# Last stage of a one-core transformer kernel: another order of its first units, registers loaded by group, gathers a unit sooner

## The reference

```python
logits = xt @ gate_w.T
scores = softmax(logits)
_, idx = top_k(scores + gate_b, 2)
weights = take_along_axis(scores, idx)             # dw: zero but for the two chosen experts
h = silu(einsum('td,eid->tei', xt, W1)) * einsum('td,eid->tei', xt, W3)     # 8 experts, 128 wide
y = einsum('tei,edi,te->td', h, W2, dw)
z = silu(xt @ Ws1.T) * (xt @ Ws3.T) @ Ws2.T        # a shared expert for all tokens
x = x + 0.5 * (y + z)
```

## Time and profile before

| | us |
|---|---|
| median of three runs | 1614.95 |
| the profiled execution, its own time | 1613.27 |
| its span from first to last instruction | 1611.3 |
| last stage, from up(0) to the end | 124 (1487.3 to 1611.3) |
| last matmul begins | 1606.4 |
| last DVE instruction ends | 1608.3 |

### The profile page before, as it was taken

One profiled execution on the slowest core, in us unless ns is written; L12 is line 12 of the kernel. 1 busy time (PEld: TensorE's weight loads), 2 busy tenths in 40 slices (PEclk: granted clock), 3 DMA queues, 4 the chain that ended last, 5 costly groups with the idle time before them and its releaser, 6 DMA issues. The chain is left out here.

```text
span 1611.3 us, 26807 instructions
## 1 busy us (share of the span) xinstructions
PE 1557.1 (97%) x9214; PEld 905.7 (56%) x9214; DVE 1245.2 (77%) x2324; ACT 1214.3 (75%) x1904; POOL 1167.9 (72%) x823
## 2 busy tenths in 40 slices
PE   3998899999999999999999999999999999999898
PEld 2566445555555555555555555555567566688575
DVE  7888777777777777777777778778888886988627
ACT  7876888989989998998898888887655543345442
POOL 0865888888888898888888888887575322476535
PEclk9999999999999999999999999999999999999999
DMA  9311879889779889879889887887401430000433
GB/s 310 128 54 41 141 140 170 144 144 180 150 151 168 155 153 168 158 144 169 164 146 165 152 159 142 159 153 137 84 1 33 129 83 4 1 1 8 107 98 98
DMA packets 641371, 197.10 MB, mean 122 GB/s; under 512 B 601547, under 2 KB 639062, under 8 KB 640982
## 3 DMA queue, kind: packets, MB, share of 16 engines
q1 hardware_dynamic: 636662, 188.19, 59.8%
q0 software_dynamic: 1536, 4.20, 0.8%
q10 hardware_dynamic: 3040, 3.02, 0.6%
HBM read 36.71 MB, written 10.22 MB: 29 GB/s over the span
## 5 line engine op out<-in xcount | busy, mean ns | idle before, releaser
L970 POOL TENSOR_TENSOR Pl<-Pm,Ph 128x1024 f16<-128x1024 f32 x256 | 545.9, 2132 | 43.8 <-ACT Ph L1311 43.5
L1301 ACT ACTIVATE Pm<-banks,nbias,s_scale 128x1024 f32<-128x1024 f32 x256 | 307.6, 1202 | 96.3 <-DVE nbias L1944 95.3
L1942 DVE TENSOR_REDUCE nmax<-banks 128x1 f32<-128x1024 f32 x256 | 311.7, 1218 | 88.3 <-PE banks L2517 87.8
L1311 ACT ACTIVATE Ph<-Pm 128x1024 f16<-128x1024 f32 x256 | 268.1, 1047 | 1.5
L949 POOL TENSOR_TENSOR rp_b<-rp_s,rope 128x512 f32<-128x512 f32 x128 | 163.1, 1274 | 98.7 <-ACT rp_s L1278 97.2
L1975 DVE SCALAR_TENSOR_TENSOR X<-banks,rinv,X 128x256 f32<-128x256 f32 x256 | 112.2, 478 | 113.0 <-PE banks L2517 113.0
L2515 PE MATMUL banks<-QK_hi 128*128 128x512 f16 x512 | 194.2, 379 | 1.6 <-DVE QK_lo L2033 0.9
L2516 PE MATMUL banks<-QK_lo,QK_hi 128*128 128x512 f16 x512 | 194.3, 379 | 0.0
L2517 PE MATMUL banks<-QK_hi,QK_lo 128*128 128x512 f16 x512 | 194.3, 379 | 0.0
L2515 PE MATMUL banks<-PT_hi,V_hi 128*128 128x512 f16 x512 | 194.0, 379 | 0.0
L2516 PE MATMUL banks<-PT_lo,V_hi 128*128 128x512 f16 x512 | 194.0, 379 | 0.0
(11 more groups left out here) (317 smaller groups left out, 3963.7 us busy)
## 6 DMA issues: line engine op xcount, KB each, us to landing
moe_raw<-in_L_ffn_W SPq DMA_DIRECT2D x48, 128.0 KB, 2.5
w_all<-in_L_attn_w_qkv SPq DMA_DIRECT2D x3, 2048.0 KB, 15.8
a_raw<-in_L_attn_w_qkv SPq DMA_DIRECT2D x24, 256.0 KB, 3.2
PT_hi<-Ph SPq DMA_TRANSPOSE x256, 3.4
PT_lo<-Pl SPq DMA_TRANSPOSE x256, 3.3
xs<-zeros SPq DMA_DIRECT2D x1, 2944.0 KB, 16.4
yd<-y_sb ACTq DMA_DIRECT2D x5, 512.0 KB, 2.9
raw_gu<-in_L_ffn_w_gate_up SPq DMA_DIRECT2D x2, 1024.0 KB, 7.3
```

Of the source, the lines that this page charges most:

```text
L970: nc.gpsimd.tensor_tensor(Pl[:, z % 4, :], Pm[:, k, :], Ph[:, z % 4, :], ALU.subtract).then_inc(pl_done.sem, 1)
L1301: nc.scalar.activation(Pm[:, k, :], two_banks[z % 2][:], ACT.Exp, bias=nbias[:, z:z + 1], scale=s_scale[:], accum_out=rsum[:, z:z + 1]).th ...
L1311: nc.scalar.activation(Ph[:, z % 4, :], Pm[:, (base * SLOTS + z) % 3, :], copy).then_inc(ph_done.sem, 1)
L1942: nc.vector.tensor_reduce(nmax[:, z:z + 1], two_banks[z % 2][:], AX, ALU.max, negate=True).then_inc(max_done.sem, 1)
```

## The change

It is a reordering. In the gathers' tables all combines and gathers come one unit sooner (tiles 0 and 1 both behind lo(15), the last two combines at unit 23). POOL runs lo(0) before the second rsqrt. ACT normalises three tiles, takes the upper part of unit 0, then the fourth tile and the rest. DVE computes each router piece before the product of its unit, the shifts and add(0) at unit 1, and the lower parts of batch 1's second half at unit 2. PE runs up(2) ahead of turn(1), down(1) ahead of the logits, and turn(1) uses banks 7 and 5. The single load of 23 registers becomes one load per group, at the head of each kind "x" unit's `up`.

```diff
-    COMBINE_AT = {**{18 + t: (t,) for t in range(TT - 2)}, 16 + TT: (TT - 2, TT - 1)}
+    COMBINE_AT = {**{17 + t: (t,) for t in range(TT - 2)}, 15 + TT: (TT - 2, TT - 1)}
-    GATHER_BEHIND = {15 + t: (t,) for t in range(TT)}
+    GATHER_BEHIND = {15: (0, 1), **{14 + t: (t,) for t in range(2, TT)}}
+    TURN_BANK = [(7, 6), (7, 5)]
...
-                rsqrt_ln(1, l, 1)
                 for i in LO_BY_POOL:
                     expert_lo(i)
+                    if i == 0:
+                        rsqrt_ln(1, l, 1)
...
                 silu(0)
-                normalise(1, l, 0)
+                normalise(1, l, 0, range(TPH - 1))
+                hi(0)
+                normalise(1, l, 0, (TPH - 1,))
                 silu(1)
-                hi(0)
                 norm_hi(0)
                 hi(1)
                 normalise(1, l, 1)
+                silu(2)
                 norm_hi(1)
+                hi(2)
...
                 for i in range(NUB):
-                    if i > DOWN_LAG:
+                    if i > DOWN_LAG + 1:
                         add(i - DOWN_LAG - 1)
-                    product(i)
-                    if i:
-                        lo(i - 1)
-                    if i == 0:
-                        shifts(1, l, 1)
-                    if i == 1:
-                        for half in range(NHALF):
-                            for c in range(DC):
-                                ln_lo_part(1, l, half, c, bank[7 - c])
-                            if half == 0:
-                                choice_weights(SORTED)
                     if i == ROUTER_AT:
                         last_shifted(1)
...
+                    product(i)
+                    if i:
+                        lo(i - 1)
+                    if i == 1:
+                        ln_lo_part(1, l, 0, 0, bank[TURN_BANK[0][0]])
+                        shifts(1, l, 1)
+                        ln_lo_part(1, l, 0, 1, bank[TURN_BANK[0][1]])
+                        choice_weights(SORTED)
+                        add(0)
+                    if i == 2:
+                        for c in range(DC):
+                            ln_lo_part(1, l, 1, c, bank[TURN_BANK[1][c]])
...
-                def load_experts():
-
+                def load_experts(g):
+
+                    tiles = range(4 * g, 4 * g + GROUP_TILES[g])
                     pe.wait_ge(router_step.sem, routed(SORTED, N_BEST + N_SECOND + N_POSITIONS))
-                    registers = [nc.tensor.alloc_register(f"expert{j}") for j in range(SLOT_TILES)]
-                    nc.tensor.reg_load(registers, eid[:])
+                    registers = [nc.tensor.alloc_register(f"expert{j}") for j in tiles]
+                    nc.tensor.reg_load(registers, eid[:, tiles[0]:tiles[-1] + 1])
...
                     if kind == "x":
+                        load_experts(g)
                         pe.wait_ge(xt_in[xt_set(g)].sem, 16 * len(XT_SETS[xt_set(g)]))
...
-                        if half:
-                            pe.wait_ge(xT_done.sem, xT_done.at(1, l * LN_GROUPS + c + 1))
+                        if half and c == 0:
+                            pe.wait_ge(xT_done.sem, xT_done.at(1, l * LN_GROUPS + 1))
+                        elif half:
+                            pe.wait_ge(x_added.sem, added_by(0))
...
                 up(0)
                 up(1)
                 turn(0)
-                load_experts()
                 down(0)
+                up(2)
                 turn(1)
-                up(2)
+                down(1)
                 last_logits(DENSE)
-                down(1)
                 up(3)
```

More of the change, by code:

```diff
@@ L1463, in rotation, with normalise @@
                                              copy).then_inc(r_qhi.sem, 1)
-            def normalise(b, l, half):
+            def normalise(b, l, half, tiles=range(TPH)):
                 act.wait_ge(ln_shift.sem, SHIFTED.index((b, l, half)) + 1)
@@ L1468, in normalise @@
                     act.wait_ge(rows_lo.sem, half + 1)
-                for t in range(half * TPH, (half + 1) * TPH):
+                for t in (half * TPH + j for j in tiles):
                     nc.scalar.activation(XN[:, t, :], X[:, b, t, :], ACT.Identity, bias=shift[:, b, t:t + 1],
@@ L1517, in norm_hi @@
                     for c in range(DC):
-                        ln_hi_part(1, l, half, c, bank[7 - c])
+                        ln_hi_part(1, l, half, c, bank[TURN_BANK[half][c]])
                 silu(0)
-                normalise(1, l, 0)
+                normalise(1, l, 0, range(TPH - 1))
+                hi(0)
+                normalise(1, l, 0, (TPH - 1,))
                 silu(1)
-                hi(0)
                 norm_hi(0)
@@ L1526, in last_experts @@
                 normalise(1, l, 1)
+                silu(2)
                 norm_hi(1)
-                for i in range(2, NUB):
+                hi(2)
+                for i in range(3, NUB):
                     if i > DOWN_LAG:
@@ L3002, in turn @@
                             pe.wait_ge(x_added.sem, x_added.at(1, RET_X + TT - 1))
-                        transpose_part(1, l, half, c, bank[7 - c])
+                        transpose_part(1, l, half, c, bank[TURN_BANK[half][c]])
                 up(0)
```

## The result

The changed kernel takes 1617.26 us, the median of 20 runs (1615.36 to 1620.0), the kernel before 1615.05 (20 runs, 1612.77 to 1616.31): a ratio of 1.0017, 95% interval 1.0011 to 1.0023. The change costs 2.2 us by the medians, 2.7 by the ratio; the prediction had +0.2, in a range that holds the result. In the profiled execution it is 1618.82 (span 1616.9) against 1613.27 (span 1611.3). Of these 5.6 us, 1.56 arise before the last stage: up(0) begins at 1488.83 in place of 1487.27. (An `up` has 12 matmuls of 512 columns, not the 24 that the description of the kernel before gives; no term of the sum uses that number.)

A forecast was written before the change was run, and what follows sets the result against it. PE, busy 97% of the span, was taken as the bound. Start -2.4, end -1.0 and loads +3.6 sum to +0.2 us on the median 1614.95, giving 1615.2 us, range 1611.7 to 1619.5.

The forecast's parts named there:

- part 2: Register loads by group: five exposed loads at the heads of up(8) to up(12) cost 3.6 us, low end 2.9.
- Rival A: Group loads at up(8) to up(12) have a large fixed cost; at 1.7 us a load, 1620 us; chance 0.2.
- rival B: Group loads are hidden by PE's queue or set 1's transfers; only -3.4 is left, 1611.5 us; chance 0.18.
- prediction's 5.0: Cost in us of the five exposed group loads if a tensor_load has the skill page's 600 ns floor; result 1616.6.
- part 1: Start, up(0) to first group: sooner last scatter brings the first group from 1522.5 to 1520.1, gain 2.4 us, low bound 1.0.
- the stop of 1.2 us: Unexplained PE stop in the logits; if it comes back before up(3), up(3) begins at 1503.9 in place of 1502.7.
- rival C: Start doesn't come sooner, through the logits' stop, new order or clock falls; gain 1.0 or less, 1616.6 us; chance 0.15.
- part 3: Gathers and combines one unit sooner: product(25) begins right after its matmuls, gain 1.0 us, bounds 0.3 and 1.1.

The follow-up runs named there:

- start-alone: Changed kernel with one register load between up(6) and down(4) and the gather and combine tables of before: 1611.46 us, ratio 0.9992 to the kernel before.
- a0: Changed kernel unaltered, run a second time: 1617.02 us, ratio 1.0012 to the kernel before.
- e3: Changed kernel with a single load of 23 registers between up(6) and down(4) in place of the six: 1613.78 us, ratio 0.9994 to the kernel before.
- a1: Changed kernel unaltered, run a third time in another set: 1618.01 us, ratio 1.0020 to the kernel before.
- e8: Changed kernel with single late register load, gather and combine tables put back as before: 1611.46 us, ratio 0.9992 to the kernel before.
- e5: Changed kernel with batch 1's logits spread inside up(3) and a single late register load: 1610.76 us, ratio 0.9989 to the kernel before.
- e4: Changed kernel with batch 1's logits spread between up(3)'s long matmuls, six loads kept: 1613.88 us, ratio 1.0008 to the kernel before.
- all-mended kernel: Changed kernel with single late load, logits inside up(3) and first output transfer held back: 1610.88 us, ratio 0.9985 to the kernel before; again 1609.96, ratio 0.9982.
- e2: Kernel before with one register load per group in place of the single load, nothing else: 1616.66 us, ratio 1.0013.
- e6: Kernel before with the new gather and combine tables, first output transfer held back until the last gather has landed: 1611.20 us, ratio 0.9993.
- tables alone: Kernel before with only the new gather and combine tables: 1613.54 us, ratio 0.9997.
- before again: Kernel before unaltered, one more execution profiled: 1614.19 us.

## Why the prediction was right, and where it wasn't

**The loads (part 2): right.** Predicted +3.6 with 2.9 as the low end. The five profiles with six loads have groups of 33.31 to 33.32, the nine with one 30.02 to 30.41, on average 30.16: +3.2. Each of the five exposed loads costs on average 0.6 to 0.65 us: 0.33 to 0.36 for the load of four registers (0.77 for the last one, of three), the rest its wait and moves, seen as idle times of up to 0.6 us at the heads of the last three units. But for that last load the duration goes nearly with the registers (23: 2.42 to 2.52 us; 4: 0.33 to 0.36), and of the 0.15 us of fixed cost assumed, (3.2 - 2.9)/5 = 0.06 is left. Rival A (a large fixed cost) and rival B (hidden) both fall. The Trainium skill, "DMA: Bandwidth & Descriptors", section "Latency and other measured facts", gives a tensor_load a floor of about 600 ns; the trace doesn't agree, with four of six loads at 0.33 to 0.36 us. The prediction's 5.0 from that page was also added up wrongly: a floor of 0.6 us leaves 81 ns a register and not 85, four then cost 0.92 and not 0.86, and the estimate by the page is 5.4, which is 2.2 too high.

**The start (part 1): every step right but one.** Moved by the 1.56 us by which the profile of after begins later, down(0) is at 1494.1 (predicted 1494.1), up(2) at 1496.2 (1496.1), down(1) at 1499.6 (1499.8), the logits at 1501.5 (1501.3). For up(3) the forecast had 1502.7, or 1503.9 if the stop of 1.2 us came back. The start-alone execution, without stops, has it at 1502.67, lo(3) at 1507.3 (predicted 1507.6) and the first group at 1519.8 (1520.1). But in the four executions with stops up(3) is put back by 1.7 to 2.1 us against the start alone (by its first matmul, or by its third where a stop stands in front of the second), where the forecast had 1.2, and in two of the four the clock then fell to half on up(3): in the profile of after 14 matmuls of 512 columns came 0.43 us apart in place of 0.21, 3.0 us, and the first group at 1523.9.

By times, the start is what is left of a kernel's difference to the one before beside it when the loads (3.2) and the end's net gain (-0.1) are taken off. In moments with stops: +2.2 - 3.2 + 0.1 = -0.9 (20 runs), a0 -0.6, e3 -0.7, a1 +0.4. In moments without: e8 -1.0, e5 -1.6, e4 -1.7, and the two timings of the all-mended kernel, whose end gains the whole 1.06, -0.5 and -1.5. Each has about 1.5 us of uncertainty (the one of 20 runs 1.0), so some -0.5 in the first case, where the change was measured, and -0.5 to -1.7 in the second. The term of -2.4 was mis-sized: this is rival C with its low bound of 1.0, and it had 0.15. What rival C named (the logits' stop, the clock in short gaps) is what happened.

The other half of the misjudgement is in the reference. I took the start of before as one number, 35.22. The same order of PE gives 35.22, 34.71 and 35.32 where the clock fell, and 32.67 where neither clock nor stops came. POOL's list is as long in both orders, so undisturbed the reorder is worth 0.2 us (32.67 to 32.50, one execution of each). What it wins beyond that is what disturbs the kernel before, and it has disturbances of its own. How often the clock falls in the kernel before isn't shown: three of four profiles have it.

One reading of the list of waits was off, without effect on the sum: of the 1.7 us of waits for sums 0.9 lie before unit 7 (0.66 and 0.25) and 0.8 at the end (0.54 and 0.28), not 1.2 and the rest.

Whether 48 matmuls of 8 columns in a row make the stops is open; in e2 they ran without a gap and the stops came behind them. What e4's expectation supposes, that PE runs ahead of the arrival of its instructions and stands until they come, would fit this and the common end of the stops, but no run tests it, and no instruction transfer is seen at that time. The four executions with the logits spread over up(3) have none, but all four ran in moments in which the compact form had none either (e6, e8, b0). For the same reason the best kernel's gain over the kernel before is shown for such moments only.

**The end (part 3): gain right, a cost missed.** Predicted -1.06 at the tail, measured -1.05 to -1.07. Combine(0) waited for its rows as predicted (0.6; 0.8 measured) at no cost. What I didn't follow is what the earlier combines release: the output transfer. The prediction follows POOL, DVE and PE there, and not SP's queue. Its price is +0.93 in the experts; holding the output back takes it away whole. In the changed kernel as repeated first, combine(4) waits 0.97 us, and so begins just ahead of a lower part on POOL:

```profile
1591.80 2.43 DVE L2317 SCALAR_TENSOR_TENSOR X<-yg,wk,X 128x256 f32<-128x256 f32 x2 [0.97 <-DMA yg<-yd,pos]
...
1592.26 1.16 POOL L1101 TENSOR_TENSOR bT_lo<-bo_h,bT_hi 128x512 f16<-128x512 f32 x1
```

The pair takes 2.43 us where it takes 1.00 elsewhere; the second instruction ends 0.8 us after POOL does. That is a delay of 0.97 + 1.43 = 2.40, with 0.95 of it in the experts. With the tables alone it is 2.26 + 0.12 = 2.38, and 0.93 come through. In the profile of after 0.68 + 1.19 = 1.87, and 0.42. In each of the three 1.45 us are absorbed by DVE's idle time and the rest stands on PE. The Trainium skill, "SBUF — State Buffer", section "Who interferes with whom", has the rule that a vector instruction with two inputs in SBUF and a GpSimd instruction that reads SBUF exclude each other. The trace agrees. I had weighed it and counted nothing, because by the rows' times no early combine met a lower part; it was the delay by the transfer that put it onto one.

**The sum** in place of -2.4 - 1.0 + 3.6 = +0.2 is -0.5 - 0.1 + 3.2 = +2.6; measured +2.2, +2.45 and +3.5. The total came out in the range, on its slow side: one cost was sized about right, and two gains were counted that executions or another queue took back. That the result lies in the range is in part luck: the range is 7.8 us wide, and the forecast's own +0.2 us lies outside the interval measured (by the ratio 1.8 to 3.7 us). Rival C, at 1616.6, describes the start better than the forecast does, and no value on record lies nearer to 1617.26.

## What to carry to other kernels

PE's list was already at its issue pace in the group units, and each load of registers added to it was paid in full: keep such loads out of such a stretch, and put one load of all where the engine waits anyway. When a step comes sooner, follow what it releases on the other queues too: here 1.07 us of gain set free an output transfer that nobody needed yet, which took 0.93 of it, and one wait on SP gave it back. And read a stage of the kernel before from several executions, of several sets: a gap that is a disturbance of most executions is a gain only on average, and an edit that was seen only in undisturbed ones isn't shown to have removed it.

## What the runs showed that I had not expected

- On the same chip the same instructions, up to the end of the start, have 0 us (e8) or 1.8 us (a1) of stops, by the set in which they ran; the kernel before is 2 us slower in the sets with stops. No semaphore and no instruction transfer in the traces explains them.
- An idle PE of 2.4 us was followed by a granted clock of 0.50 at once (before, tables alone), by 0.54 only about a microsecond later (before again), or by no fall (output held back, with 0.71 us of busy PE in the 2 us from 1496). In the changed kernel the fall came behind the stops, after 0.47 us of busy PE in 2 us, and in three other executions with stops (a0, e3 and, in another order, e2) it didn't.
- A gather's rows landed after 5.4 us in place of 2.4 when a 512 KB write started 0.2 us behind it.
- Register loads: 23 take 2.42 to 2.52 us, four take 0.33 to 0.36, but the first four, ahead of the wait for the first group's data, took 0.51 to 0.52, and the last load, of three, 0.77, in each of the five profiles with six loads.
